# Third layer's feature attention: GpSimd sums four rounds before TensorE takes them in

## The reference, cut to what matters

```python
def _softmax_kernel(x, R):
    n = jnp.sqrt(jnp.sum(x * x, axis=-1, keepdims=True))
    x = x / jnp.maximum(n, 1e-06)
    p = jnp.einsum('...d,ed->...e', x, R)
    feats = jnp.concatenate([jnp.sin(p), jnp.cos(p)], axis=-1)
    return feats / math.sqrt(F)
...
k = jnp.repeat(k, rep, axis=1)          # 8 heads of keys and values, 16 of queries
v = jnp.repeat(v, rep, axis=1)
qp = _softmax_kernel(q, rand_matrix)
kp = _softmax_kernel(k, rand_matrix)
kv = jnp.einsum('bhsf,bhsd->bsfd', kp, v)      # summed over the heads h
out = jnp.einsum('bhsf,bsfd->bhsd', qp, kv)
out = out.reshape(b, s, HID)
return out @ Wo.T + bo
```

## Time and profile before

| | us |
|---|---|
| median of 3 runs | 1616.43 |
| lowest and highest of them | 1613.71, 1619.91 |
| the profiled execution's own time | 1623.54 |
| its span in the trace | 1621.7 |
| PE busy, of the span | 1140.4 |
| DVE busy, of the span | 1059.8 |
| POOL busy, of the span | 575.6 |

### The profile page before, as it was taken

The page is one execution under the profiler, slowest core; times in us unless marked ns, Lnnn a source line. Parts: engine busy times, 40 slices in busy tenths (PEclk is TensorE's granted clock), DMA queues, the critical chain, the costliest instruction groups (busy, mean ns, idle before and its releaser), DMA issues. The chain is left out here.

```text
span 1621.7 us, 21361 instructions
## 1 busy us (share of the span) xinstructions
PE 1140.4 (70%) x6058; PEld 718.6 (44%) x6058; DVE 1059.8 (65%) x1790; ACT 492.7 (30%) x949; POOL 575.6 (35%) x596
## 2 busy tenths in 40 slices
PE   7445547999309695554998896699847878866970
PEld 3211235777004572122565644577634324445860
DVE  6999975773695557998885683320345878745454
ACT  3423322333402252332211200343313346622430
POOL 0046613552755113662000042023440632204746
PEclk9769987999659898998999888799978859987985
DMA  5074347996321403433300432142520140048944
GB/s 189 31 255 148 114 137 225 306 315 228 95 68 33 125 4 130 155 130 133 117 1 0 120 77 37 43 144 77 173 85 7 30 129 3 3 125 249 329 137 123
DMA packets 138562, 195.87 MB, mean 121 GB/s; under 512 B 35408, under 2 KB 98914, under 8 KB 137196
## 3 DMA queue, kind: packets, MB, share of 16 engines
q1 hardware_dynamic: 104316, 145.85, 29.0%
q0 software_dynamic: 12704, 29.36, 6.3%
q10 hardware_dynamic: 21456, 19.60, 3.9%
HBM read 142.80 MB, written 31.72 MB: 108 GB/s over the span
## 5 line engine op out<-in xcount | busy, mean ns | idle before, releaser
L165 POOL TENSOR_SCALAR rstd<-moments 128x4 f32<-128x4 f32 x24 | 6.5, 270 | 410.1 <-DVE moments L148 410.1
L177 PE MATMUL psum<-w_ident,h 128*128 128x128 f32 x144 | 29.8, 389 | 110.6 <-DVE h L155 110.6
L558 PE MATMUL psum<-l1s_read,w_ident 128*128 128x512 f32 x128 | 64.9, 630 | 53.5 <-DVE l1s_read L623 53.4
L558 PE MATMUL psum<-l0s_read,w_ident 128*128 128x512 f32 x128 | 65.4, 636 | 52.2 <-DVE l0s_read L623 52.2
L1906 DVE TENSOR_REDUCE l3x_neg<-psum 128x2 f32<-128x512 f32 x128 | 80.7, 683 | 23.9 <-PE psum L1777 23.9
L1881 ACT ACTIVATE l3x_work<-psum 128x512 f32<-128x512 f32 x128 | 72.5, 598 | 50.9 <-PE psum L1800 50.6
L546 POOL TENSOR_TENSOR l1s_drive<-l1s_du,l1s_bc 128x1024 f32<-128x1024 f32 x32 | 75.3, 2355 | 35.3 <-DVE psum L619 35.3
L546 POOL TENSOR_TENSOR l0s_drive<-l0s_du,l0s_bc 128x1024 f32<-128x1024 f32 x32 | 75.2, 2353 | 35.3 <-DVE psum L619 35.3
L177 PEld LDWEIGHTS psum<-w_ident,h 128*128 128x128 f32 x144 | 25.4, 202 | 117.6 <-DVE h L155 115.3
L1162 PE MATMUL psum<-l0f_w_in,l0f_xT 128*128 (+1 forms) x224 | 76.8, 466 | 0.0
L1037 POOL DMA_INDIRECT l3f_x<-l3f_h_rows,l3f_token_of x64 | 59.3, 927 | 48.5 <-DVE l3f_token_of L1433 28.5
(11 more groups left out here) (642 smaller groups left out, 3131.1 us busy)
## 6 DMA issues: line engine op xcount, KB each, us to landing
l0f_w_in<-in_l0f_w_in SPq DMA_DIRECT2D x56, 352.0 KB
l0s_bc<-l0s_scratch SPq DMA_DIRECT2D x16, 1024.0 KB, 5.1
l1s_bc<-l1s_scratch SPq DMA_DIRECT2D x16, 1024.0 KB, 5.2
l3f_w_in<-in_l3f_w_in SPq DMA_DIRECT2D x32, 384.0 KB
l0f_w_down<-in_l0f_w_down SPq DMA_DIRECT2D x56, 176.0 KB
l2f_w_in<-in_l2f_w_in SPq DMA_DIRECT2D x24, 352.0 KB
l0f_y_rows<-l0f_y ACTq DMA_DIRECT2D x56, 128.0 KB
l3f_w_down<-in_l3f_w_down SPq DMA_DIRECT2D x32, 192.0 KB
```

The source lines that it names most:

```text
L177: ins = nc.tensor.transpose(m.psum[:, at:at + P], m.h[:, t, k * P:(k + 1) * P], m.ident[:])
L558: ins = nc.tensor.matmul(m.pair(2 + c)[:, cols], lhsT=m.ident[:], rhs=rhs[:, cols], start=start, stop=stop, skip_group_check=True)
```

## The change

GpSimd now adds four rounds instead of two: two additions of pairs as before, and a third that adds the two sums. TensorE takes in only that sum of four, so that there are four `add`s of eight matmuls in place of eight. The tiles of weighted values (`mixed`) are eight in place of four: the four of before, and four that lie over tiles whose contents are no longer needed at that point (`rot0`, `rot1`, `whole`, `sq_k0`). `mix(s)` waits for an `add` from step 8 on in place of step 4. TensorE's `add(u)` stands behind `weigh(4u + 5)`, and the last at the end.

```diff
@@ -2108,6 +2108,8 @@
     mixed = [m.sb(tag + f"mixed{i}", [P, KD, HALF]) for i in range(4)]
+    mixed += [a[:].rearrange("p b s -> p (b s)").rearrange("p (c t) -> p c t", c=KD) for a in tmp]
+    mixed += [a[:].rearrange("p (c t) -> p c t", c=KD) for a in (whole, sq["k0"])]
@@ -2154,10 +2156,13 @@
             norm_gpsimd(m, pool, n)
-            for u in range(STEPS // 2):
-                pool.wait_ge(mix_done, 2 * u + 2)
-                first = mixed[2 * u % 4]
-                nc.gpsimd.tensor_tensor(first[:], first[:], mixed[2 * u % 4 + 1][:], ALU.add).then_inc(paired, 1)
+            for u in range(STEPS // 4):
+                four = mixed[4 * u % 8:4 * u % 8 + 4]
+                for i in (0, 2):
+                    pool.wait_ge(mix_done, 4 * u + i + 2)
+                    nc.gpsimd.tensor_tensor(four[i][:], four[i][:], four[i + 1][:], ALU.add).then_inc(paired, 1)
+                pool.wait_ge(paired, 3 * u + 2)
+                nc.gpsimd.tensor_tensor(four[0][:], four[0][:], four[2][:], ALU.add).then_inc(paired, 1)
@@ -2203,13 +2208,13 @@
             def add(u):
-                h, first = divmod(u, STEPS // 4)
-                pe.wait_ge(paired, u + 1)
+                h, first = divmod(u, STEPS // 8)
+                pe.wait_ge(paired, 3 * u + 3)
                 for t in range(4):
                     for c in range(KD):
                         ins = nc.tensor.matmul(m.pair(h)[:, t * D + c * P:t * D + (c + 1) * P],
-                                               lhsT=mixed[2 * u % 4][:, c, t * P:(t + 1) * P], rhs=m.ident[:], start=(first == 0 and c == 0 and t % 2 == 0),
-                                               stop=(first == STEPS // 4 - 1), skip_group_check=True)
+                                               lhsT=mixed[4 * u % 8][:, c, t * P:(t + 1) * P], rhs=m.ident[:], start=(first == 0 and c == 0 and t % 2 == 0),
+                                               stop=(first == STEPS // 8 - 1), skip_group_check=True)
                 ins.then_inc(added, 1)
@@ -2233,9 +2238,9 @@
             for s in range(STEPS):
                 weigh(s)
-                if s % 2 and s >= 3:
-                    add((s - 3) // 2)
-            add(STEPS // 2 - 1)
+                if s % 4 == 1 and s > 4:
+                    add((s - 5) // 4)
+            add(STEPS // 4 - 1)
@@ -2258,7 +2263,7 @@
             def take_sums(h):
-                act.wait_ge(added, (h + 1) * STEPS // 4)
+                act.wait_ge(added, (h + 1) * STEPS // 8)
@@ -2321,9 +2326,9 @@
-                if s >= 4:
-                    dve.wait_ge(added, (s - 4) // 2 + 1)
-                nc.vector.tensor_tensor(mixed[s % 4][:], weights_ps[s % 2],
+                if s >= 8:
+                    dve.wait_ge(added, (s - 8) // 4 + 1)
+                nc.vector.tensor_tensor(mixed[s % 8][:], weights_ps[s % 2],
```

## The result

The changed kernel takes 1640.71 us (median of 5 runs, 1636.73 to 1641.54) against 1616.73 for the one before (5 runs, 1613.71 to 1620.03): a ratio of 1.0132, interval 1.0109 to 1.0155, slower. (The ratio is estimated over all runs; the quotient of the two medians is 1.0148, inside the interval.) A second series of the same kernel gave 1640.61 against 1620.63, ratio 1.0119 (1.0096 to 1.0141). Forecast were slower, 1631.4, and a range up to 1638: the direction was right and the size was not.

The account below looks back on a forecast made before the run. The prediction took VectorE and GpSimd taking turns on a shared path as the bound, TensorE nearly level. Path 11.9, last `add` at half clock 1.8 and other falls 1.3 summed to 15.0 us: 1631.4, range 1624 to 1638.

Parts of the forecast that it names:

- What bounds the loop: Steady loop: `mix`, `by_heads` and GpSimd's addition in turn take 5.56 us per two steps; TensorE needs 5.49, nearly level.
- Rivals 1 and 2: 1: TensorE the bound, a gain, 1611.3, 3 in 100; 2: additions and `by_heads` not exclusive, 1624.4, 8 in 100.
- 5: Rival 5: something later takes the delay up and the kernel stays within 0.5%; 5 in 100.
- Who goes first: On the shared path `by_heads(6)`, which asked 1.2 us earlier, goes ahead of GpSimd's sum of four.
- rival 3: GpSimd keeps its turn for the third addition and `by_heads(6)` waits through both: 1629.3; 13 in 100.
- The path of 11.9 us: Longer rounds and a second addition behind `mix(15)` make the last `add` start 11.9 us late, carried to the end.
- The last `add` at half clock: After a 6.3 us wait TensorE's clock has fallen, so the last `add` costs 1.8 us more.
- I take 1.3, half of one fall: Clock cost of TensorE's three 3.8 us waits: 1.3 us taken; at most 2.7 per fall, 8.1 for three.
- One of the signs of being wrong: TensorE's `weigh`s of twice the length in every round would show the prediction wrong.
- Rival 4: TensorE's clock falls in every wait: 11.9 + 1.8 + 8.1 = 21.8 us, 1638.2; 16 in 100.
- The range of the main case: The prediction's own case, at 55 in 100, was given 1626 to 1634.

Follow-up runs that it names:

- no_third: The changed kernel without GpSimd's third addition, so TensorE leaves two steps of every four out of the result: ratio 1.0013, stage +1.5 us.
- extra_addition: The kernel before plus one unused GpSimd addition on dead tiles behind every second pair addition: ratio 1.0031, stage +2.3 us.
- psum_queries: The changed kernel with `by_heads(2)` to `by_heads(7)` reading a free PSUM pair in place of the query rows in SBUF: ratio 1.0063, stage +13.7 us.
- busy_waits: The changed kernel plus unused constant matmuls in TensorE's waits, 3 ahead of `add(0)` to `add(2)`, 6 ahead of the last: ratio 1.0081, stage +11.6 us.
- late_add: The changed kernel with each `add` moved from behind `weigh(4u + 5)` to behind `weigh(4u + 7)`: ratio 1.0057, stage +5.9 us.
- after_again: The changed kernel run once more, unchanged, for a second profile and more times: ratio 1.0119, stage +19.7 us.

## Why the prediction was right in its direction and wrong in its size

- *What bounds the loop.* Right. `mix`, `by_heads` and GpSimd's addition in turn set 5.56 us for two steps; no_third shows that TensorE's 99% were no bound, extra_addition and psum_queries that the shared path is one. Rivals 1 and 2 fall, and so does 5: the medians of the whole execution lie 24.0 and 20.0 us apart.
- *Who goes first.* Right: `by_heads(6)` went ahead of the sum, so rival 3 falls. The Trainium skill's rule (SBUF — State Buffer, "Who interferes with whom") agrees with this trace: held from 946.35, `by_heads` took its turn at 947.51, and the sum, which asked at 947.58, waited.
- *The path of 11.9 us.* Right within half a us: busy_waits, at full clock, has `mix(3)` to the last `add` in 992.03 - 944.52 = 47.5 us, against 36.1 before: 11.4. By rounds that is 2.9, 2.9 and 3.3 us (3.0, 3.0 and 3.5 forecast) and 2.4 ahead of the last `add` (2.4). Of the first two, 1.0 each is the third addition (late_add against before) and 1.8 the `weigh`s behind the `add` (busy_waits against late_add). The waits were 3.5 and not 3.8 us, as `weigh(5)` ended 0.2 us later and the sum 0.1 earlier than forecast.
- *The last `add` at half clock.* Right: 1.8 us forecast, 3.78 - 2.05 = 1.7 measured.
- *The clock in the other waits: the step that failed.* The term "I take 1.3, half of one fall", bounded at 2.7 for each of three, measured 7.3. `mix(3)` to the last `add` takes 997.77 - 942.95 = 54.8 us in the changed kernel and 47.5 in busy_waits: 7.3 us. The fall came with every wait of 3.5 us, 3 of 3, again 3 of 3 in after_again, and 2 of 2 in psum_queries. The size of a single fall was right within 0.3 us (1.65, 2.74 and 2.93 us by rounds, the last two over the bound), and its frequency was not. One of the signs of being wrong that the prediction names came in part: the `weigh`s behind an `add` took 4.3 to 4.8 us, not 3.6, in every round. Rival 4, which had 16 in 100, is what happened: 21.8 forecast, 19.5 measured in the stage. The difference is the path (0.5), the falls (0.8) and a tail that is 1.0 shorter (its last matmuls, 5.51 us, ran partly at full clock; before 6.53).
- *The rows chosen for it.* I had weighed one wait of 3.0 without a fall against one of 2.6 with one, and taken that as even odds for a wait of 3.8 us, longer than both. The Trainium skill, "TensorE: Matmul & The Clock Gate", section "HAM oscillation — how this bites in real kernels", told of a fall in each of a series of waits between short bursts of work. Here some 12 us of work lie between two waits, and this trace shows the same, 3 of 3.
- The stage's 19.5 us against medians 24.0 and 20.0 us apart: both intervals hold 19.5, and what is over it in the first series is not assigned to anything. The stage alone, laid on the 1616.43 of the forecast, would give 1635.9.
- *The range.* The range of the main case was drawn tighter than its own terms: 11.9 + 1.8 + two falls of 2.7 + 1.5 for the spread reach 1637.0, not 1634, and rival 4, at 1638.2, lies beyond the 1638 that was said to take in most of it.

## What to carry to other kernels

An engine at 99% can have a partner path of the same length: add up the loop's period from each engine's own instructions before taking load off one, and look at whether an instruction that starts early ends late because another engine holds what it reads. Work moved between engines changes where the receiving one must wait, and in a list that is executed in order the whole list waits there, so place the taker of a later result later. If a change opens repeated waits of some 3.5 us in a matmul loop, count a fall of the clock for each, not half of one for all: here the falls made this stage 7.9 of its 19.5 us longer (9.0 up to the end of the last `add`, part of which came back in a shorter tail).

## What the runs showed of the hardware

A `tensor_tensor` on VectorE with both inputs in SBUF and an addition on GpSimd exclude each other for the whole instruction (1.21 becomes 2.24, 2.34 becomes 3.27); with one of VectorE's inputs in PSUM neither is longer (1.21 and 2.35). TensorE's clock fell in or just behind 8 of 8 waits of 3.5 us ahead of an `add` (in three of the eight about 0.9 to 1.5 us into the `add`), behind 1 of 3 of 2.65, and behind none of 1.75 or less; one fall cost 1.6 to 3.0 us. That the falls of one kernel cost so unlike amounts, and that equal waits of 2.65 us ended both ways in one loop, was not expected, and what decides it stays open. Filling waits with matmuls whose result is thrown away made a stage 7.9 us shorter.
